# Last mixture-of-experts stage of a four-block model: the search's counts, the second bias and the spread of products over search steps are changed

## The reference

```python
def balanced_assignment(scores):          # scores: 4096 tokens x 8 experts
    C = T // E                            # 512 tokens for each expert
    for e in range(E):
        s = jnp.where(taken, -jnp.inf, scores[:, e])
        _, idx = jax.lax.top_k(s, C)      # the 512 best that are still free
        taken = taken.at[idx].set(True)
...
h = layer_norm(routed, ln_g, ln_b)        # routed: 8 x 512 x 256
h = jax.nn.gelu(jnp.einsum('ecd,edf->ecf', h, w1) + b1[:, None, :])   # f = 1024
h = jnp.einsum('ecf,efd->ecd', h, w2) + b2[:, None, :]
out = routed + h
```

## Time and profile before

| | |
|---|---|
| median of 3 runs | 3332.83 us (3326.93 to 3336.69) |
| profiled execution: its own time | 3330.74 us |
| profiled execution: span | 3329.0 us |
| mean granted TensorE clock | 0.904 of full speed |
| busy over the span: PE, PEld, DVE, ACT, POOL | 81%, 48%, 59%, 48%, 29% |
| last stage: first compare of the search, last indirect store issued | 2917.23, 3320.08 us |

### The profile page before, as it was taken

The page is one execution under the profiler, slowest core; times in us unless marked ns, Lnnn a source line. Parts: engine busy times, 40 slices in busy tenths (PEclk is TensorE's granted clock), DMA queues, the critical chain, the costliest instruction groups (busy, mean ns, idle before and its releaser), DMA issues. The chain is left out here.

```text
span 3329.0 us, 62821 instructions
## 1 busy us (share of the span) xinstructions
PE 2685.7 (81%) x16332; PEld 1589.0 (48%) x16333; DVE 1965.9 (59%) x4549; ACT 1609.3 (48%) x2512; POOL 968.8 (29%) x1660
## 2 busy tenths in 40 slices
PE   8699999999987289964899596888888878628877
PEld 5333333333335278844688443444444435415554
DVE  3478888788757733346433363667776745456640
ACT  3277777777777234333333253566666653302112
POOL 1411111111116345520355364222222204303333
PEclk9699999999999589975899898999999996659999
DMA  6500010101006012232122284111111104322231
GB/s 166 177 20 19 19 24 14 26 13 26 19 4 196 15 56 67 67 106 72 46 70 68 75 226 128 24 26 26 26 26 26 26 24 137 115 74 83 92 100 62
DMA packets 365545, 215.06 MB, mean 65 GB/s; under 512 B 284766, under 2 KB 345698, under 8 KB 364647
## 3 DMA queue, kind: packets, MB, share of 16 engines
q1 hardware_dynamic: 235688, 110.84, 12.4%
q10 hardware_dynamic: 111808, 50.34, 5.3%
q0 software_dynamic: 17920, 52.46, 5.0%
HBM read 129.13 MB, written 85.98 MB: 65 GB/s over the span
## 5 line engine op out<-in xcount | busy, mean ns | idle before, releaser
L339 ACT ACTIVATE att_pr<-att_S 128x1024 f32<-128x1024 f32 (+1 forms) x896 | 835.9, 941 | 426.1 <-ACTq L346 423.2
L379 DVE TENSOR_REDUCE att_mparts<-att_S 128x2 f32<-128x1024 f32 x640 | 776.9, 1225 | 168.8 <-DVEq L375 165.1
L255 PE MATMUL att_S<-att_qT,att_kT 64*128 64x512 f32 (+3 forms) x1792 | 429.8, 472 | 45.3 <-PEq L250 44.1
L271 PE MATMUL att_OP<-att_pr,att_vn 128*32 128x512 f32 (+3 forms) x3584 | 450.8, 564 | 1.0 <-PEq L265 0.7
L243 PE MATMUL att_S<-att_kT,att_qT 64*128 64x512 f32 (+3 forms) x1792 | 390.3, 430 | 75.7 <-PEq L237 65.9
L255 PEld LDWEIGHTS att_S<-att_qT,att_kT 64*128 64x128 f32 x1792 | 174.7, 184 | 470.0 <-issue 458.8
L179 POOL COPY att_vn<-att_raw 128x256 f32<-128x256 f32 x64 | 25.4, 398 | 1147.9 <-POOLq L178 1147.9
L243 PEld LDWEIGHTS att_S<-att_kT,att_qT 64*128 64x128 f32 x1792 | 187.8, 190 | 174.5 <-issue 168.6
L385 DVE CUSTOM_DVE_ANT_0 att_unused<-att_S,att_mask 128x128 f32<-128x128 f32 (+3 forms) x512 | 228.3, 488 | 69.6 <-DVEq L375 69.6
L1257 POOL DMA_INDIRECT experts_xs<-scaled,ffn_source x144 | 140.5, 975 | 316.9 <-PEq L1288 143.8
L1354 DVE COPY experts_y<-experts_Y 128x256 f32<-128x256 f32 x144 | 61.1, 424 | 220.7 <-DVEq L1353 220.7
(11 more groups left out here) (317 smaller groups left out, 4907.2 us busy)
## 6 DMA issues: line engine op xcount, KB each, us to landing
qkv<-qkv_y ACTq DMA_DIRECT2D x64, 384.0 KB, 3.3
att_raw<-qkv SPq DMA_DIRECT2D x96, 256.0 KB, 3.3
rows<-post_rows ACTq DMA_DIRECT2D x32, 384.0 KB, 2.8
ffn_w<-in_w ACTq DMA_DIRECT2D x12, 1024.0 KB
ao<-att_aon SPq DMA_DIRECT2D x32, 256.0 KB, 2.9
post_at<-ao SPq DMA_DIRECT2D x64, 128.0 KB, 3.1
rms_rows<-mixed SPq DMA_DIRECT2D x32, 256.0 KB, 3.6
qkv_rows<-mixed SPq DMA_DIRECT2D x32, 256.0 KB, 2.9
```

The costliest lines, as they stand in the source:

```text
L255: mm=pe.matmul(S[:,b,h,f:512],kT[r,s,kt*128:kt*128+128],qT[r,s,c*512+f:c*512+512],start=True,stop=not diag)
L271: mm=pe.matmul(OP[32*j:32*j+32,f:512],vn[:,s,kt,h,:],pr[:,n%4,h,f:512],start=kt<2,stop=g in last_groups,skip_group_check=True)
L339: nc.scalar.activation(pr[:,n%4,:,f:512],S[:,ring["e",n],:,f:512],ACT.Exp,scale=exp_scale).then_inc(s_free[ring["e",n]],1)
L379: nc.vector.tensor_reduce(mparts[:,s,:,2*qt+half],S[:,b,:,0:width(qt,half)],AX.X,ALU.max).then_inc(end,1)
```

## The change

Three things change in `assigned_experts`. First, VectorE no longer sums over the tiles before the count: `ge` is written in bf16, TensorE multiplies it with the ones in four products of 120 columns (15 candidates x 8 tiles) that add up in `CN`, and VectorE sums the remaining 8 columns of each candidate from `CN` into `total` behind the count. Second, the product of ones with `b2` goes; `b2` is loaded into all 128 partitions (1 MB instead of 8 KB), GpSimd adds it to `xs` part 1 in place (`with_bias`, four additions for each expert, behind `final(e-1,0)`, and for expert 0 behind its gather), and `sum_tile` waits for that. Third, the pieces are shared over the search steps by their columns, and tiles 0 and 1 are summed one step later, in steps 5 and 6.

```diff
-cand=...; ge=m.sb("ge",[128,CANDS,NT]); part=m.sb("part",[128,CANDS],BF)
+cand=...; ge=m.sb("ge",[128,CANDS,NT],BF); total=m.sb("total",[128,CANDS])       # CHUNK=8
-b2=m.sb("b2",[1,EXPERTS*DIM]); ones=m.sb("ones",[1,128])
+b2=m.sb("b2",[128,EXPERTS*DIM])
 @block.gpsimd
+                def with_bias(e):
+                    pool.wait_ge(x_loaded[e%2],16*T4*(e//2+1))
+                    for t in range(T4):
+                        nc.gpsimd.tensor_tensor(xs[:,e%2,t,1],xs[:,e%2,t,1],b2[:,e*DIM:e*DIM+DIM],ALU.add).then_inc(biased,1)
+                pool.wait_ge(consts,16*6)
                 gather(0)
+                with_bias(0)
                 for e in range(1,EXPERTS+1):
                     if e<EXPERTS: gather(e)
                     for t in range(T4+1):
                         if t<T4: given(e-1,t)
                         if t>=1: final(e-1,t-1)
+                        if t==1 and e<EXPERTS: with_bias(e)
 @block.sync
-                sp.dma_start(b2[:],b2_d.rearrange("(o d) -> o d",o=1)).then_inc(consts,16)
+                sp.dma_start(b2[:],b2_d.partition_broadcast(128)).then_inc(consts,16)
 @block.tensor
-                    if c<FC: pe.matmul(Y[:,t%2,0:DIM],hT[:,c,128*t:128*t+128],w2[:,e%2,c,:],start=c==0,stop=False)
-                    else: pe.matmul(Y[:,t%2,0:DIM],ones[:],b2[:,e*DIM:e*DIM+DIM],start=False,stop=True).then_inc(y_full,1)
-                PIECES=1+KC*FC+(FC+1)*T4
+                    mm=pe.matmul(Y[:,t%2,0:DIM],hT[:,c,128*t:128*t+128],w2[:,e%2,c,:],start=c==0,stop=c==FC-1)
+                    if c==FC-1: mm.then_inc(y_full,1)
+                PIECES=1+KC*FC+FC*T4
                 def count():
                     pe.wait_ge(part_ready,1).then_inc(part_ready,-1)
-                    pe.matmul(CN[:,0:CANDS],tri[:,1,:],part[:],start=True,stop=True).then_inc(count_full,1)
+                    for j in range(NT//CHUNK):
+                        mm=pe.matmul(CN[:,0:CANDS*CHUNK],tri[:,1,:],ge[:,:,CHUNK*j:CHUNK*j+CHUNK],start=j==0,stop=j==NT//CHUNK-1)
+                    mm.then_inc(count_full,1)
+                def share(l):
+                    columns=[CAP]*(KC*FC+1-HEAD)+[DIM]*(FC*T4)
+                    return HEAD+sum(sum(columns[:i+1])*LEVELS<=sum(columns)*l for i in range(len(columns)))
...
-                        if e>=2: pieces(e-2,HEAD+(PIECES-HEAD)*l//LEVELS,HEAD+(PIECES-HEAD)*(l+1)//LEVELS)
+                        if e>=2: pieces(e-2,share(l),share(l+1))
 @block.vector
+                    dve.wait_ge(biased,T4*e+t+1)
                     done(V.tensor_tensor(o[:,t],Y[:,t%2,0:DIM],xs[:,e%2,t,1],ALU.add))
-                SUMS={0:3,4:0,5:1,7:2}
+                SUMS={0:3,5:0,6:1,7:2}
-                            red(part[:],ge[:],ALU.add)
                         dve.sem_inc(part_ready,1)
...
                         dve.wait_ge(count_full,1).then_inc(count_full,-1)
-                        ts(ok[:],CN[:,0:CANDS],float(CAP),float(2**bit),ALU.is_ge,ALU.mult)
+                        red(total[:],CN[:,0:CANDS*CHUNK].rearrange("p (c t) -> p c t",c=CANDS),ALU.add)
+                        ts(ok[:],total[:],float(CAP),float(2**bit),ALU.is_ge,ALU.mult)
```

More of the change, by code:

```diff
@@ L1506, in assigned_experts @@
 def assigned_experts(nc,tag,scores,rows_d,tri_d,cand_d,marks_d,w1_d,w2_d,b1_d,b2_d,out_d,ident_d):
-    T4=CAP//128; FC=F1//128; FAR=1.5e38; A,B=32,16
+    CHUNK=8; T4=CAP//128; FC=F1//128; FAR=1.5e38; A,B=32,16
     with Mem(nc,tag) as m:
@@ L1516, in assigned_experts @@
         bound=m.sb("bound",[128,NT]); s=m.sb("s",[128,NT]); P=m.sb("P",[128,1],I32); msk=m.sb("msk",[128,1],I32)
-        cand=m.sb("cand",[128,2,CANDS],I32); base=m.sb("base",[128,CANDS],I32); ge=m.sb("ge",[128,CANDS,NT]); part=m.sb("part",[128,CANDS],BF)
+        cand=m.sb("cand",[128,2,CANDS],I32); base=m.sb("base",[128,CANDS],I32); ge=m.sb("ge",[128,CANDS,NT],BF); total=m.sb("total",[128,CANDS])
         ok=m.sb("ok",[128,CANDS]); found=m.sb("found",[128,1],I32)
@@ L1524, in assigned_experts @@
         hot_ready=m.sem("hot_ready"); table_full=m.sem("table_full"); table_ready=m.sem("table_ready"); token_loaded=[m.sem(f"token_loaded{e}") for e in range(EXPERTS)]
-        ident=m.sb("ident",[128,128]); b1=m.sb("b1",[128,EXPERTS,FC]); b2=m.sb("b2",[1,EXPERTS*DIM]); ones=m.sb("ones",[1,128])
+        ident=m.sb("ident",[128,128]); b1=m.sb("b1",[128,EXPERTS,FC]); b2=m.sb("b2",[128,EXPERTS*DIM])
         w1=m.sb("w1",[128,2,KC,F1]); w2=m.sb("w2",[128,2,FC,DIM]); xs=m.sb("xs",[128,2,T4,3,DIM]); xT=m.sb("xT",[128,KC,CAP]); hT=m.sb("hT",[128,FC,CAP])
@@ L1531, in assigned_experts @@
         tx_full=m.sem("tx_full"); xT_ready=m.sem("xT_ready"); h_full=m.sem("h_full"); hT_ready=m.sem("hT_ready")
-        y_full=m.sem("y_full"); y_free=m.sem("y_free"); o_done=m.sem("o_done"); var=m.sem("var"); half_done=m.sem("half_done"); pool_done=m.sem("pool_done")
+        y_full=m.sem("y_full"); y_free=m.sem("y_free"); o_done=m.sem("o_done"); var=m.sem("var"); half_done=m.sem("half_done"); pool_done=m.sem("pool_done"); biased=m.sem("biased")
         root_ready=m.sem("root_ready"); ln_ready=m.sem("ln_ready"); o_free=m.sem("o_free"); fin_stored=[m.sem(f"fin_stored{t}") for t in range(T4)]
@@ L1603, in pieces @@
                         elif n<=KC*FC: first(e,(n-1)//KC,(n-1)%KC)
-                        else: second(e,(n-1-KC*FC)//(FC+1),(n-1-KC*FC)%(FC+1))
+                        else: second(e,(n-1-KC*FC)//FC,(n-1-KC*FC)%FC)
                 def count():
                     pe.wait_ge(part_ready,1).then_inc(part_ready,-1)
-                    pe.matmul(CN[:,0:CANDS],tri[:,1,:],part[:],start=True,stop=True).then_inc(count_full,1)
+                    for j in range(NT//CHUNK):
+                        mm=pe.matmul(CN[:,0:CANDS*CHUNK],tri[:,1,:],ge[:,:,CHUNK*j:CHUNK*j+CHUNK],start=j==0,stop=j==NT//CHUNK-1)
+                    mm.then_inc(count_full,1)
                 def ranks(e):
@@ L1663, in _ @@
                 done(V.tensor_copy(tri[:],trif[:]))
-                done(V.memset(ones[:],1.0))
                 dve.sem_inc(tri_ready,1); dve.sem_inc(o_free,T4)
@@ L1711, in search @@
                         tt(ge[:],s[:].rearrange("p (o t) -> p o t",o=1).broadcast_to([128,CANDS,NT]),here.bitcast(F32).rearrange("p (c o) -> p c o",o=1).broadcast_to([128,CANDS,NT]),ALU.is_ge)
-                        with nc.allow_low_precision("counts up to 32 are exact"):
-                            red(part[:],ge[:],ALU.add)
                         dve.sem_inc(part_ready,1)
```

## The result

The changed kernel takes 3350.77 us (median of four runs, 3347.68 to 3357.14); the kernel before, on the same chip, 3331.05 (four runs, 3326.93 to 3336.69). The ratio is 1.0062, with an interval of 1.0044 to 1.0081: slower, by 19.7 us. Predicted were 3347 and a range of 3334 to 3361.

What follows compares the result with a forecast made beforehand. Bound: the dependence chain in two searches, then VectorE and TensorE alternately, with turns; TensorE's pieces and turn waits behind the last. 2.6 - 1.3 + 0.1 + 10.7 + 3.1 = +15.2 us; forecast 3347, range 3334 to 3361.

Steps and rivals of the forecast that it cites:

- b2: Head of the last stage: loading 1 MB ahead of the weights delays VectorE's first instruction, +2.6 us.
- The counts: First two searches: a shorter VectorE reduction against four TensorE products for one, together -1.3 us.
- A step that is only the chain: Search step where VectorE has no other work between compare and count: changes by +0.01 us at the slow clock.
- The rival of the weight loads: Four products of a count don't hide their loads: +0.3 on 56 counts, 17 us, 3364; chance 0.08.
- The turn: Between searches: four additions, 3.0 us, delay given 2, ScalarE's copies and the firsts; largest term, +10.7 us.
- the one that set the contention aside: Additions inside the searches fall where VectorE is ahead of TensorE, so sharing SBUF with GpSimd costs nothing.
- the idle, predicted at 3.4 us: At a turn: TensorE idles 3.4 us, and the clock behind it adds 1.7 to every turn.
- an idle of 1 us at the turns: Sign that the forecast is wrong; the right sign was TensorE idle 3 to 4 us ahead of the firsts.
- The first step: First step of a search behind a turn: takes 9.6 us, where it is now 6.98.
- Step 4: Searches 3 to 7: the new share of TensorE work makes it 5.9 us instead of 5.10, a loss of 0.7.
- The rival of more slow clocks in the searches: Step 2 idles 1.7 us, step 3's firsts run slow: +1.7 in five searches, 3355; chance 0.17.
- Behind the last search: Bias products saved -7.4, GpSimd's pace +0.9, two turns' idle +6.2 and clock +3.4: +3.1 us.

Runs made afterwards that it cites:

- e2_bias: The kernel before with only the second bias changed (GpSimd adds b2 from 128 partitions, no product of ones): 3350.42 us, ratio 1.0067.
- e4_late: The changed kernel with the four b2 additions moved behind final 3 instead of behind final 0: 3332.84 us, ratio 1.0010 to the kernel before.
- e7_late_tt: e4_late plus four spare GpSimd additions of b2 to itself where the change has its additions: 3363.76 us, ratio 1.0094 to the kernel before.
- e3_share: The kernel before with only the share by columns and the later tile sums: 3341.04 us, ratio 1.0039.
- e5_late_b2: e4_late with b2 loaded behind the weights on its own semaphore that only GpSimd waits for: 3334.86 us, ratio 1.0002 to the kernel before.
- e6_best: e5_late_b2 with the old share by number and the old places of the sums: 3318.74 us, ratio 0.9960 to the kernel before.
- e11_old_share: The changed kernel with the old share by number and old sums, additions and b2 load left in place: 3352.79 us, ratio 1.0059 to the kernel before.
- e9_delay: e4_late with GpSimd only waiting for a small load where the change has its additions: 3342.03 us, ratio 1.0020 to the kernel before.
- e8_late_ms: e4_late plus three spare GpSimd memsets of 128x1024 where the change has its additions: 3365.78 us, ratio 1.0093 to the kernel before.
- e1_counts: The kernel before with only the counts changed (four products, sum of 8 behind the count): 3323.76 us, ratio 0.9985.
- e10_behind2: The changed kernel with the additions behind given 2 and ahead of final 1: 3337.55 us, ratio 1.0009 to the kernel before.

## Why the prediction was right, and which of its steps were not

**The sign, the size and the main cause were right.** The additions between `final` 0 and `given` 2 cost more than all else saves. e2_bias has the loss, e4_late takes 17 us of it away by the place alone, and the firsts start at +13.9 us after step 6's compare, for a predicted 13.8. That the total came out within 4 us of the 3347 is luck in part: several terms were off by 3 to 7 us, some up and some down, as follows.

**b2.** +2.9 us (6.06 to 8.97), predicted +2.6; in the last 3 us of that wait the DMAs moved 388 GB/s, the figure taken.

**The counts.** A step that is only the chain went from 3.10 to 3.05 us (predicted +0.01), a covered one gained 0.37 (4.47 to 4.10, 4.86 to 4.49; predicted 0.38), searches 1 and 2 gained 1.1 (predicted 1.3). That agreement hides a term that the prediction left out: without step 7 of the second search they gained 2.0, and there 0.9 was lost, since the additions for expert 0 fall beside its selection (`bound` 0.72 and `s` 0.54 us for 0.19 each). The rival of the weight loads is out: four products take 0.56 us at the low clock and 0.37 at full, where the prediction's working by columns gives 0.56 and 0.36. In searches 3 to 7 step 1 gained 0.3 to 2.1 and step 2 0.4 to 0.7, more than predicted, but not by the counts: e2_bias, with the old counts, gained 4.1 us in these steps, the changed kernel 7.5, and e4_late, with the new counts and the turns in time, only 0.3. In the runs these steps are short where the first step before them was long; so part of a late turn's cost comes back there, which the prediction didn't have.

**The turn: the date of the firsts held, two of its parts failed.** The failed step is the one that set the contention aside, "by this trace they fall where VectorE is ahead of TensorE (the turn), and cost nothing". They fall beside step 7, on which the rank products wait. `ok`, `P` and `flags` took 0.60 + 1.36 + 0.69 us where e4_late shows 0.17 + 0.16 + 0.39: 1.9 us, and with it the rank products came at +11.0 instead of +9.3. The Trainium skill, in "GPSIMD Engine Reference", Key points, names two cases in which the engines contend for SBUF: VectorE in a 2-port perf mode, or with two SBUF inputs. The prediction told only the second. For `P`, which has two, this trace agrees (0.16 to 1.36). `ok`, with one SBUF tensor as input, was held too (0.60, and 2.41 in e7_late_tt); whether that is the first case no run here shows. The second part is the idle, predicted at 3.4 us: it was 0.9 to 1.8, since 2.4 of it had moved ahead of the rank products. The prediction had named an idle of 1 us at the turns as a sign of being wrong, and by that sign this part of it was. The first step, which the idle lengthens, came out at 8.85 in three searches and 9.64 in the fourth, for 9.6, and step 7 at 9.8 for about 7.9. Because the firsts wait for ScalarE too, one error nearly paid for the other: the two steps together took 18.6 us in those three, and 17.5 had been predicted; over all searches they took 14.1 us more than before, where the prediction's terms give 9.8. How near it was is in TensorE's idle ahead of the firsts: 0.88 and 1.03 us in two of the five turns, about the 0.87 that e7_late_tt has when the rank products come last, and 1.39 to 1.78 in the other three, where `given` 2 came last. So in three turns and behind the last search the predicted chain decides, and in the other two the held VectorE is as late as it.

**Step 4: a rival that was given 0.17.** I took 5.9 us for it (0.8 more than 5.10, of which the sum had 0.7), and in three searches of five it took 6.10 to 6.12. In the other two it took 8.85 at half the clock, and the sum of the five is +10.4 instead of +3.5. The rival of more slow clocks in the searches said this with another place: it had step 3's firsts slow, behind an idle of 1.7 in step 2. That idle came (1.77 us at 3040.66), and eight instructions behind it still took 3.66. The clock fell one step later, behind the 1.49 of step 3, in two searches; in the other three it stayed full behind the same idle. e3_share shows the slow step 4 without the other changes, at 12 us, e5_late_b2 against e6_best at 14. Step 4 was the term furthest off, by 7 us. In the total it was hidden: steps 1 to 3 gained 5 us more than predicted, and the costs of the parts don't add. Alone they are -5, +21 and +12, 28 us, and together 20; and e11_old_share, without the division by columns, gets nothing back. So the division costs 12 to 14 us where the turns are in time, and nothing measurable where they are late.

**Behind the last search.** +6.5 for +3.1. The bias product was worth more: four tiles' seconds take 14.05 us, 3.51 a tile, where one took 3.72 + 0.62 = 4.3 with its bias; that is 0.8 a tile instead of 0.62, and some -9.3 us instead of -7.4. The idle was mis-sized a little (4.46 for 4.0 and 3.54 more than before each, +7.1), the clock behind it by nearly half (3.0 a turn instead of 1.7, +6.0). I had read 1.7 from eight instructions behind an idle of 1.74, and the low clock lasts longer behind 4.46. GpSimd's pace of 4.22 us added 1.5 (predicted 0.9), and expert 5's turn idles 1.2 more, which the prediction left out.

**What stays open.** How the loss at the turns beside the searches divides between delay and contention at the change's full 2.8 us: e9_delay has too short a delay, e7_late_tt and e8_late_ms have both effects, and no run holds VectorE ahead of the rank products with `given` 2 in time. Why e7_late_tt costs 28 us where the change's additions cost 17 isn't settled either. Its `ok` took 2.41 us where the change's took 0.60, though both began 0.63 ahead of the run's recorded start; but from the first compare to the last store's start the two profiled executions take nearly the same, 424.3 us in e7_late_tt and 425.1 in the changed kernel, against 401.2 in e4_late. And no run tells when the clock falls: an idle of 1.96 us was followed by 5.37 for eight instructions in e1_counts and by 3.67 in e6_best.

## What to carry to other kernels

Before filler work goes onto an engine that looks idle, look up what stands behind it in that engine's order and who waits for that: here the same instructions cost 17 us more ahead of `given` 2 than at the end of the round. Work moved to GpSimd is also paid by VectorE where the two run side by side: next to nothing behind the rank products (e10_behind2), but at the turns of e7_late_tt, where the rank products wait for VectorE, it is what holds TensorE. A step that becomes longer can give part of it back in the next ones, so a part of a change is judged over the whole round. Equal shares of columns are not equal steps: a share has to be laid beside the waits of its step, and a step that leaves TensorE idle just ahead of a wait can cost the clock as well.

## What the runs showed of the hardware

- One VectorE instruction of 128x15, 0.17 us alone, took 2.41 us beside four GpSimd additions in a row (2.31) and 3.38 beside three memsets (2.74): it was held for nearly the whole run, even by instructions that only write. VectorE's sums of a tile (0.42 and 0.43 us) beside the same additions were not held. Instructions of two inputs beside such a run took 0.53 instead of 0.19, or 1.36 instead of 0.16.
- Behind an idle of 4.46 us, 32 instructions of the firsts took 17.0 us instead of 13.97, and behind 1.66 in e4_late still 13.97; behind 2.45 in e9_delay 13.97 once and 15.67 once. In the searches an idle of 1.49 with one of 1.11 behind it came with a clock of 0.62 in one search and with full clock in another.
- A product with one row of weights and 256 columns (two instructions) took 0.62 us from its start to the next product's, one with 128 rows 0.46; taking it away shortened a tile by 0.8.
